# Exchanging two steps of ScalarE, relu and a small square root, in the expert loops of a mixture-of-experts kernel

## The chip, the cores and the metric
One core of one Trainium2 chip runs the whole program. The metric is the device time of one execution in microseconds, the median of several runs. The engines are TensorE (PE), VectorE (DVE), ScalarE (ACT), GpSimd (POOL) and SyncE (SP). Each goes through its own list of instructions in order; they are tied together by semaphores, which one engine raises and another waits for.

## The reference
The program is a layer of three stages on x of 8 x 256 tokens with 128 features: half an expert layer, an attention, and again half an expert layer (the same weights):

```python
x = x + 0.5 * ffn(layernorm(x))
x = x + attn(layernorm(x))
x = x + 0.5 * ffn(layernorm(x))
```

The expert layer has 8 experts, each token goes to the best 2 of them:

```python
h = relu(xt @ W1[e] + b1[e])            # 128 -> 512
h = layernorm(h) * g1[e] + be1[e]
y = relu(h @ W2[e] + b2[e])             # 512 -> 128
y = layernorm(y) * g2[e] + be2[e]
out = sum over the 2 experts of gate * y
```

All is float32. Each of the two normalisations needs 1 / sqrt(variance + eps) for each token. The square root is taken by ScalarE, the reciprocal by VectorE.

## The kernel before
**Tiles and pairs.** Tokens are sorted by expert into 39 tiles of 128 rows, each of one expert. Two tiles make a pair; there are 20 pairs (the last has one tile). Buffers are doubled: pair n uses slot u = n % 2. Both expert layers ("f1", first, and "f2", last) run this way. f1 does pair 0 and 1 by hand, pairs 2 to 15 in a hardware loop of two pairs a round (seven rounds), and pairs 16 to 19 unrolled. f2 has its first six pairs woven into the end of the attention by a hand-written order of their own (which the change doesn't touch), then the loop for pairs 6 to 15 (five rounds) and again 16 to 19 unrolled.

**What happens to a pair.** PE turns the two tiles of x (`turn_x`, line 829), multiplies by W1 (`hidden`, line 840, into PSUM), turns the relu's result in eight pieces (`turn_h`, line 849), and multiplies by W2 (`second`, line 858, 16 matmuls into bank 7). ScalarE evacuates PSUM and takes the roots: `copy_xT` (684), `relu` (691, one instruction of 1024 columns for the pair), `copy_hT` (697), `sqrt1` (701, the root of the variance of h), `sqrt2` (705, that of y), and `finish` (712, the last scaling of y into `yo`, two instructions). VectorE takes the statistics of the relu (`stats1`, 1192, two instructions; `moments1`, 1199), adds up y (`y_sums`, 1206 and 1209), clips y at zero and takes its statistics (`y_stats`, 1215 to 1221), and normalises it (`y_norm`, 1231 and 1233). In f1 SP stores `yo` and POOL gathers the tiles of x to come; in f2 SP loads the tiles and POOL scatters `yo`.

**The orders.** Each engine's order within one body is written by hand. For body n they are:

- PE: turn_h(n), turn_x(n+2), hidden(n+1), second(n)
- VectorE: moments1(n), y_sums(n-1), y_stats(n-1), y_norm(n-1), stats1(n+1)
- ScalarE: copy_hT(n), copy_xT(n+2), sqrt1(n), sqrt2(n-1), relu(n+1), finish(n-1)

**The waits around the change.** relu(n+1) waits for `h` (hidden(n+1) done), for `hTp` (turn_h(n-1) done, since it overwrites what was turned) and for `bn` (stats1(n-1) done). sqrt2(n-1) waits for `mv2` (y_stats(n-1) done). y_norm(n-1) waits for `sq2` (sqrt2(n-1)); finish(n-1) for `yz` (y_norm(n-1)) and for the store of two pairs ago; stats1(n+1) and turn_h(n+1) for `relu`. second(n) waits for `hTc` (copy_hT(n)) and for `ya` (y_sums(n-1) done, which frees bank 7). In f2 hidden(n+1) waits for relu(n), as there is but one set of banks for h; in f1 there are two.

At the head of a loop's round PE and VectorE read the numbers of the round's experts from SBUF into registers (`experts`, line 58); on PE this stands between the last matmul of second and the first wait of turn_h.

Of the kernel before, what the change touches and what calls it, by code (L numbers as in the profile page):

```python
# [106 lines left out]
def build(nc, x, Wq, Wk, Wv, Wo, lq1, lk1, lq2, lk2, Wr, br, W1, b1, g1, be1, W2, b2, g2, be2, out, stages=("f1", "at", "f2")):  # L107
    with ExitStack() as ctx:
# [433 lines left out]
        def turned_rows(act, S, g, first):  # L542

            act.wait_ge(S["xnTp"], g + 1)
            if g == 3:
                act.wait_ge(S["lgp"], 1)
            act.copy(turned_slot(g), turn_bank(g)[:].rearrange("p (a b) -> p a b", a=4)).then_inc(S["xnTc"], 1)
# [107 lines left out]
        def own_rows(act, h):  # L655

            act.wait_ge(s_wmix, h + 1)
            for a in range(4):
                e = 4 * h + a
                last = act.activation(wmix[0:16, e * DIM:(e + 1) * DIM], bank[6 + h][0:16, a * DIM:(a + 1) * DIM], ACT.Copy,  # L660
                                      scale=mask16[:, e:e + 1])
            last.then_inc(s_mixed, 1)

        def own_bias(act, a, b):
            for t in range(a, b):
                last = act.activation(be2x[:, t, :], be2p[:], ACT.Copy, scale=own_t[:, t:t + 1])
            last.then_inc(s_be2x, 1)

        def deviations(act, S, g, n=2):
            a, b = n * g, n * g + n  # L670
            act.wait_ge(S["mv"], b)
            act.activation(sdev[:, a:b], mv[:, a:b, 1], ACT.Sqrt, bias=eps_c[:]).then_inc(S["sd"], 1)
# [44 lines left out]
        def moe_scalar(act, S, first):  # L717
            if first:
                act.activation(spad, eps_c[:], ACT.Sqrt)

            if first:
                deviations(act, S, 0, 4)
                for g in range(1, 4):
                    deviations(act, S, g, 4)
                    turned_rows(act, S, g - 1, first)
                    if g == 1:
                        act.wait_ge(s_cols, 1)
                        act.copy(cols[:], bank[6][:, 0:96]).then_inc(s_colc, 1)
                        act.wait_ge(s_cols, 2)
                        act.copy(be2p[:], bank[7][:, 0:DIM]).then_inc(s_colc, 1)  # L730
                turned_rows(act, S, 3, first)
                hidden_weights_back(act, range(0, 3))
                act.wait_ge(s_ld_w2, 16)
                w2g = w2c[:].rearrange("p (a d) -> p a d", d=DIM)
                w2v = w2s[:].rearrange("p a c d -> p (a c) d")

                def scaled(h):
                    for a in range(16 * h, 16 * h + 16):
                        last = act.activation(w2g[:, a, :], w2v[:, a, :], ACT.Copy, scale=cols[:, a:a + 1])
                    last.then_inc(s_w2g, 1)  # L740

                scaled(0)
                hidden_weights_back(act, range(3, 6))
                scaled(1)
                act.wait_ge(S["top"], 1)
                act.activation(gden[:], mw[:], ACT.Exp).then_inc(S["gexp"], 1)
                act.wait_ge(A["lam"], 1)
                act.activation(lam_e[:], lam_s[:], ACT.Exp).then_inc(A["lame"], 1)
                act.activation(spad, eps_c[:], ACT.Sqrt)
                act.wait_ge(s_const, NCONST)  # L750
                own_rows(act, 0)
                hidden_weights_back(act, range(6, 8))

            def gates_turned():
                act.wait_ge(S["gTp"], 1)
                act.copy(gsT[:], gates_bank(first)).then_inc(S["gTc"], 1)

            if first:
                gates_turned()
            copy_xT, relu, copy_hT, sqrt1, sqrt2, finish = scalar_pair(act, S, first)  # L760

            def body(n, u, kx=2, kh=2, k=2, lag=True):
                copy_hT(n, u, k)
                if kx:
                    copy_xT(n + 2, u, kx)
                sqrt1(n, u, k)
                if lag:
                    sqrt2(n - 1, 1 - u)
                if kh:
                    relu(n + 1, 1 - u, kh)  # L770
                if lag:
                    finish(n - 1, 1 - u)

            if first:
                copy_xT(0, 0)
                own_rows(act, 1)

                def own_b2(h):
                    act.wait_ge(s_b2m, h + 1)
                    act.copy(b2p[:, 512 * h:512 * h + 512], bank[6 + h][:]).then_inc(s_mixed, 1)  # L780

                own_b2(0)
                relu(0, 0)
                own_b2(1)
                copy_xT(1, 1)
                own_bias(act, 0, 4)
                body(0, 0, lag=False)
                own_bias(act, 4, 10)
                body(1, 1)
                own_bias(act, 10, 16)  # L790
            with act.Fori(1 if first else AHEAD // 2, PAIRS // 2 - 2) as i:
                for u in range(2):
                    body(i * 2 + u, u)
            left = [min(2, max(0, SLOT_TILES - 2 * p)) for p in range(PAIRS + 2)]
            for n in range(PAIRS - 4, PAIRS):
                body(n, n % 2, kx=left[n + 2], kh=left[n + 1], k=left[n])
                if n >= LATE and first:
                    act.wait_ge(S["xnTp"], n - LATE + 5)
                    act.copy(late_oT[:, n - LATE].rearrange("p n e -> p (n e)"), bank[LATE_BANKS[n - LATE]][:, 0:LATE_TILES * P]
                             ).then_inc(S["xnTc"], 1)  # L800
            sqrt2(PAIRS - 1, (PAIRS - 1) % 2, left[PAIRS - 1])
            finish(PAIRS - 1, (PAIRS - 1) % 2, left[PAIRS - 1])
            if not first:
                gates_turned()
                gate_diagonals(act, (4, 5, 12, 13))
# [482 lines left out]
        def gates_bank(first):  # L1288
            return bank[5 if first else 1][:, 0:P]

        def gate_diagonals(eng, tiles):

            eng.wait_ge(sems["f2"]["gsum"], 1)
            for t in tiles:
                for k in range(TOPK):
                    g = gate[:, k, t:t + 1]
                    if eng is nc.scalar:
                        last = eng.activation(diag8[:, diag_at(t), k, :], ident[:], ACT.Copy, scale=g)
                    else:
                        last = eng.tensor_scalar(diag8[:, diag_at(t), k, :], ident[:], g, None, ALU.mult)  # L1300
            last.then_inc(s_diag, 1)
# [827 lines left out]
        def hidden_weights_back(act, experts_):  # L2129
            for e in experts_:  # L2130
                act.wait_ge(s_cols, 2 + e + 1)
                act.activation(w1s[:, e * FF:(e + 1) * FF], bank[W1_BANKS[e % 3]][:], ACT.Copy, scale=1.0 / P).then_inc(s_colc, 1)
# [165 lines left out]
```

## Time and profile before
| | |
|---|---|
| runs | 487.77, 489.46, 494.69 us (median 489.46) |
| profiled execution | span 487.7 us; no other time is given for it |
| PE busy | 424.1 us (87%), weight loads 289.9 us |
| VectorE busy | 351.3 us (72%) |
| ScalarE busy | 291.3 us (60%) |
| POOL busy | 255.2 us (52%) |
| line 691 (relu) | 40 instructions, 39.5 us |
| line 705 (sqrt2) | 40 instructions, 11.8 us; idle ahead of them 36.3 us, 25.6 of it until line 1221 of VectorE |
| chain that ended last | PE 44%, VectorE 19%, issue 14%, ScalarE 13% |

The busy share of an engine is over the whole span. "Idle ahead" is time in which the engine had nothing to do just before those instructions, and what is named with an arrow is what ended it, inferred from the semaphores. The chain that ended last is followed back from the last instruction. The f1 loop lies between 60 and 131 us, its unrolled pairs up to 149 us, the f2 loop between 400 and 447 us and its unrolled pairs up to 467 us.

### The profile page before, as it was taken

How to read it: one execution, taken by the hardware profiler on the slowest of the kernel's cores; microseconds unless marked ns; L12 is line 12 of the kernel's file. 1: busy time of each engine (PE TensorE's matmuls, PEld its weight loads, DVE VectorE, ACT ScalarE, POOL GpSimd, SP SyncE). 2: the span in 40 equal slices, each digit the busy share in tenths (PEclk: the TensorE clock that was granted, in tenths of full speed). 3: DMA queues.
4: the chain of work that ended last, by engine and by line, in shares of the span. 5: the costliest groups of instructions: out<-in, count | busy, mean ns of one | idle time of the engine just before them, and what ended most of it. 6: DMA issues, size and time to landing. Idle time of an engine off the chain costs nothing.

```text
span 487.7 us, 11940 instructions
## 1 busy us (share of the span) xinstructions
PE 424.1 (87%) x3686; PEld 289.9 (59%) x3693; DVE 351.3 (72%) x1291; ACT 291.3 (60%) x591; POOL 255.2 (52%) x355
## 2 busy tenths in 40 slices
PE   7999999999999678889897878786899689999883
PEld 7654667777776335556465554554566457776633
DVE  5874677877877595788967776555576848887765
ACT  2395876666654437778585757543755356676540
POOL 8684634343633567256473754546524828545430
PEclk9898999999999979999999989869899979999999
DMA  7901143354422101000000000101111111211017
GB/s 233 341 19 34 31 149 135 135 203 164 135 110 88 32 23 34 12 12 13 23 13 23 23 18 29 32 15 32 52 45 40 60 39 55 59 54 49 29 46 242
DMA packets 26001, 35.18 MB, mean 72 GB/s; under 512 B 4297, under 2 KB 18689, under 8 KB 24802
## 3 DMA queue, kind: packets, MB, share of 16 engines
q1 hardware_dynamic: 21010, 24.68, 15.3%
q0 software_dynamic: 4944, 9.90, 7.1%
q8 instruction: 26, 0.43, 0.4%
q14 instruction: 21, 0.17, 0.1%
HBM read 15.45 MB, written 18.30 MB: 69 GB/s over the span
## 4 chain that ended last, share of the span: by engine, by line
PE 44%; DVE 19%; issue 14%; ACT 13%; DMA 4%; DVEq 2%; SPq 1%; POOL 1%; another core or an unknown queue 1%; POOLq 0%; ACTq 0%
PE bank L840 5%; PE bank L858 4%; DVE mx L1930 4%; ACT wide L691 4%; ACT early L1488 3%; DVE st L1192 3%; PE bank L849 3%; PE bank L1684 2%; PE bank L1692 2%; ACT wide L1480 2%; PE bank L2126 2%; PE bank L1641 2%; PE bank L1702 2%; PE bank L1777 2%; PE bank L1663 2%
## 5 line engine op out<-in xcount | busy, mean ns | idle before, releaser
L858 PEld LDWEIGHTS bank<-w2c,hT 128*128 128x128 f32 x624 | 75.3, 194 | 27.0 <-issue 26.7
L858 PE MATMUL bank<-w2c,hT 128*128 x624 | 78.0, 278 | 6.4 <-ACT hT L697 3.3
L840 PE MATMUL bank<-w1s,xT 128*128 x156 | 75.9, 608 | 1.1 <-DVE w2c L2144 0.6
L1930 DVE TENSOR_REDUCE mx<-bank 128x4 f32<-128x1024 f32 (+1 forms) x48 | 58.6, 1221 | 21.8 <-PE bank L1672 17.9
L1488 ACT ACTIVATE early<-bank 128x768 f32<-128x768 f32 x64 | 51.8, 813 | 36.7 <-PE bank L1692 36.1
L484 POOL DMA_INDIRECT xgw<-xn_scratch,slot_u x39 | 37.1, 952 | 53.2 <-PE bank L829 43.2
L455 POOL DMA_INDIRECT y_scratch<-yo,dest_u x39 | 39.0, 1001 | 40.1 <-ACT yo L712 32.8
L1192 DVE BATCH_NORM_STATS2 st<-wide 128x6 f32<-128x512 f32 x78 | 50.1, 683 | 10.6 <-ACT wide L691 9.0
L697 ACT COPY hT<-bank 128x1024 f32<-128x1024 f32 (+1 forms) x40 | 39.5, 988 | 22.2 <-PE bank L849 19.7
L433 POOL DMA_INDIRECT xr_scratch<-row_buf,hi_i x32 | 31.9, 998 | 31.8 <-DVE hi_i L644 12.9
L849 PE MATMUL bank<-ident,wide 128*128 128x128 f32 x312 | 41.8, 276 | 5.2 <-ACT wide L691 4.2
L691 ACT ACTIVATE wide<-bank 128x1024 f32<-128x1024 f32 (+1 forms) x40 | 39.5, 988 | 8.1 <-PE bank L840 8.1
L849 PEld LDWEIGHTS bank<-ident,wide 128*128 128x128 f32 x312 | 34.2, 141 | 9.7 <-ACT wide L691 6.6
L840 PEld LDWEIGHTS bank<-w1s,xT 128*128 128x128 f32 x156 | 27.1, 194 | 21.1 <-issue 21.1
L1480 ACT COPY wide<-bank 128x1024 bf16<-128x1024 bf16 x32 | 32.2, 1014 | 8.9 <-PE bank L1641 8.8
L1361 POOL DMA_INDIRECT yk<-y_scratch,posi x28 | 28.0, 999 | 17.4 <-DMA yk<-y_scratch,posi 6.3
L1209 DVE SCALAR_TENSOR_TENSOR yy<-bank,r,b2p 128x128 f32<-128x128 f32 x78 | 24.7, 351 | 14.6 <-DVE r L1206 10.0
L705 ACT ACTIVATE sd<-mv,eps_c 128x2 f32<-128x2 f32 (+1 forms) x40 | 11.8, 296 | 36.3 <-DVE mv L1221 25.6
L1684 PE MATMUL bank<-mxT,sel 64*128 64x384 bf16 x128 | 22.6, 350 | 9.7 <-ACT early L1488 7.0
L712 ACT ACTIVATE yo<-yz,r 128x128 f32<-128x128 f32 x78 | 27.1, 394 | 5.7 <-DVE yz L1233 3.5
L1430 POOL TENSOR_TENSOR orr<-oms,neg_half 128x16 f32<-128x16 f32 x7 | 20.5, 2932 | 9.7 <-DVE oms L1967 9.5
L1663 PE MATMUL bank<-mrhs,mlhs 64*128 64x128 bf16 (+1 forms) x192 | 15.9, 246 | 10.6 <-DVE mx L1930 6.5
(360 smaller groups left out, 931.5 us busy)
## 6 DMA issues: line engine op xcount, KB each, us to landing
xr_scratch<-row_buf SPq DMA_DIRECT2D x8, 1032.0 KB
xgw<-xr_scratch SPq DMA_DIRECT2D x39, 64.5 KB
y_scratch<-yo SPq DMA_DIRECT2D x19, 128.0 KB
w1s<-in_L_ffn_W_dram SPq DMA_DIRECT2D x1, 2048.0 KB, 9.9
early<-y_scratch SPq DMA_DIRECT2D x8, 256.0 KB, 3.5
xn_scratch<-row_buf SPq DMA_DIRECT2D x1, 1024.0 KB
out_dram<-xs SPq DMA_DIRECT2D x8, 128.0 KB, 2.3
row_buf<-row_buf SPq DMA_DIRECT2D x6, 128.0 KB
```

What stands on the lines that cost most here:

```text
L455: pool.indirect_dma_start(out=y_dram, out_offset=bass.IndirectOffsetOnAxis(ap=dest_u[:, 2 * p + j:2 * p + j + 1], axis=0), in_=yo[:, p % 2 ...
L484: pool.indirect_dma_start(out=xg[:, u, :], out_offset=None, in_=xn_dram, in_offset=bass.IndirectOffsetOnAxis(ap=slot_u[:, n:n + 1], axis=0 ...
L691: act.activation(hh[:, u, 0:k, :], banks[:, h_at[u]:h_at[u] + k, :], ACT.Relu).then_inc(S["relu"], 1)
L697: act.copy(hT[:, u, 0:k, :], banks[:, 5:5 + k, :]).then_inc(S["hTc"], 1)
L840: last = pe.matmul(bank[h_at[u] + j][:], xT[:, u, j, :], w1s[:, bass.ds(e * FF, FF)], start=True, stop=True)
L849: last = pe.transpose(bank[5 + j][:, c * P:c * P + P], hh[:, u, j, c * P:(c + 1) * P], ident[:])
L858: last = pe.matmul(bank[7][:, j * DIM:(j + 1) * DIM], hT[:, u, j, c * P:(c + 1) * P], w2c[:, bass.ds(e * (FC * DIM) + c * DIM, DIM)], star ...
L1192: last = dve.bn_stats(st1[:, u, j, :], hh[:, u, j, :])
L1480: act.copy(dst[:, slot, :, u * P:u * P + P], src.bitcast(BF16).rearrange("p (a e) -> p a e", e=P)).then_inc(A[name + "Tc"], 1)
L1488: act.activation(prob[:, g], quad[:, low:low + 2, 0:3 * P], ACT.Exp).then_inc(A["prob"], 1)
L1684: pe.matmul(o, sel[r:r + 64, g:g + 1].to_broadcast([64, P]), mxT[r:r + 64, :], start=True, stop=False)
L1930: dve.tensor_reduce(mx[:, c:c + 2 * per].rearrange("p (a q) -> p q a", q=2), quad[:, low:low + 2, :].rearrange("p q (a e) -> p q a e", a=p ...
```

## The change
In the body that ScalarE runs for each pair, relu(n+1) goes ahead of sqrt2(n-1), and stands directly behind sqrt1(n). The orders of the other engines, all waits and all instructions stay as they are.

```diff
                 sqrt1(n, u, k)
-                if lag:
-                    sqrt2(n - 1, 1 - u)
                 if kh:
                     relu(n + 1, 1 - u, kh)
                 if lag:
+                    sqrt2(n - 1, 1 - u)
                     finish(n - 1, 1 - u)
```

`lag` is false in body 0 of f1 alone, `kh` is the number of tiles of pair n+1 and is 0 in the last body. Both steps stand together in bodies 1 to 18 of f1 and 6 to 18 of f2.

## Rows read from the trace of the kernel before

**Rows 1.** Windows, 69 to 130 us: length, then busy us: PE, PEld, DVE, ACT, POOL.
```profile
69.00:130.00 61.00, 58.12 (x372) 44.63 (x371) 48.21 (x209) 40.56 (x86) 23.70 (x28) 1.00 0.49 165
```

**Rows 2.** Timeline of ScalarE, first loop; start us, duration us, engine, line, operation.
```profile
104.71 0.30 ACT L705 ACTIVATE sd<-mv,eps_c 128x2 f32<-128x2 f32 x1 [0.80 <-DVE mv L1221]
104.91 1.00 ACT L691 ACTIVATE wide<-bank 128x1024 f32<-128x1024 f32 x1
...
109.67 0.29 ACT L705 ACTIVATE sd<-mv,eps_c 128x2 f32<-128x2 f32 x1 [1.09 <-DVE mv L1221]
109.88 1.00 ACT L691 ACTIVATE wide<-bank 128x1024 f32<-128x1024 f32 x1
110.83 0.69 ACT L712 ACTIVATE yo<-yz,r 128x128 f32<-128x128 f32 x2
```

**Rows 3.** Timeline of PE, same stretch, without weight loads.
```profile
102.37 1.88 PE L840 MATMUL bank<-w1s,xT 128*128 x4
104.09 1.95 PE L858 MATMUL bank<-w2c,hT 128*128 x16
105.97 1.09 PE L849 MATMUL bank<-ident,wide 128*128 128x128 f32 x8
...
108.84 1.95 PE L858 MATMUL bank<-w2c,hT 128*128 x16
111.23 0.95 PE L849 MATMUL bank<-ident,wide 128*128 128x128 f32 x7 [0.44 <-ACT wide L691]
```

**Rows 4.** Timeline of VectorE, same stretch.
```profile
105.23 0.61 DVE L1233 SCALAR_TENSOR_TENSOR yz<-yy,mv,g2b 128x128 f32<-128x128 f32 x2
105.95 1.28 DVE L1192 BATCH_NORM_STATS2 st<-wide 128x6 f32<-128x512 f32 x2
...
107.88 0.63 DVE L1209 SCALAR_TENSOR_TENSOR yy<-bank,r,b2p 128x128 f32<-128x128 f32 x2 [0.31 <-DVE r L1206]
...
109.49 0.15 DVE L1221 BATCH_NORM_AGGREGATE mv<-st 128x2 f32<-128x6 f32 x1
...
110.10 0.61 DVE L1233 SCALAR_TENSOR_TENSOR yz<-yy,mv,g2b 128x128 f32<-128x128 f32 x2
110.91 1.28 DVE L1192 BATCH_NORM_STATS2 st<-wide 128x6 f32<-128x512 f32 x2 [0.20 <-ACT wide L691]
```

**Rows 5.** Timeline of VectorE, end of the first loop.
```profile
130.16 0.94 DVE L1233 SCALAR_TENSOR_TENSOR yz<-yy,mv,g2b 128x128 f32<-128x128 f32 x2
131.03 0.68 DVE L1192 BATCH_NORM_STATS2 st<-wide 128x6 f32<-128x512 f32 x1
```

**Rows 6.** Timeline of ScalarE, four relus: two of the first loop, two of the last.
```profile
69.85 1.00 ACT L691 ACTIVATE wide<-bank 128x1024 f32<-128x1024 f32 x1
...
129.94 1.00 ACT L691 ACTIVATE wide<-bank 128x1024 f32<-128x1024 f32 x1
...
417.08 1.00 ACT L691 ACTIVATE wide<-bank 128x1024 f32<-128x1024 f32 x1
...
446.60 1.01 ACT L691 ACTIVATE wide<-bank 128x1024 f32<-128x1024 f32 x1
```

**Rows 7.** Timeline of PE, last loop, where PE has no gaps.
```profile
402.07 1.95 PE L858 MATMUL bank<-w2c,hT 128*128 x16
...
406.66 1.95 PE L858 MATMUL bank<-w2c,hT 128*128 x16
408.45 0.82 PE L849 MATMUL bank<-ident,wide 128*128 128x128 f32 x6
```

**Rows 8.** Timeline of PE, last loop, at a loop head.
```profile
425.89 1.95 PE L858 MATMUL bank<-w2c,hT 128*128 x16
428.05 0.52 PE L849 MATMUL bank<-ident,wide 128*128 128x128 f32 x3 [0.21 <-ACT wide L691]
```

**Rows 9.** Waits of PE, 60 to 141 us; us in total, times, longest us.
```profile
PE bank L849 <- ACT wide L691: 3.4, 7, 0.8
```

**Rows 10.** Waits of all engines, 407 to 448 us.
```profile
POOL y_scratch L455 <- ACT yo L712: 13.0, 7, 2.1
```

## The prediction
> **What bounds the kernel now.** Times are of one profiled execution with a span of 487.71 us; the three runs shown are 487.77, 489.46 and 494.69 us, so the span stands beside the lowest and 1.7 us under the median. I work out a difference on the trace and put it on the median.
>
> First the page's busy shares: TensorE (PE) is the busiest engine, 87% of the span. The stretch from 69 to 130 us lies inside the first expert loop, and there PE is busy for 58.1 of 61 us [rows 1]: whatever is moved on the other engines can bring little unless PE's own gaps close. Then the timeline of one round (two pairs), engine by engine. I call "h" the product of W1, "relu" line 691, "sqrt2" line 705, "stats1" line 1192 and "second" the product of W2, line 858.
>
> ScalarE: sqrt2 starts at 104.71 after 0.80 us of idleness, relu follows 0.20 later at 104.91 [rows 2]. PE: h of that pair starts at 102.37 and takes 1.88, so it is there at 104.25 [rows 3]. So relu stands 0.66 us behind a square root whose input comes late. No table load lies between the two: they start 0.20 apart [rows 2], so their exchange costs none. VectorE: the chain that sets the pace. stats1 starts at 105.95, the sums of y (line 1209) end at 107.88 + 0.63 = 108.51, the moments of y end at 109.49 + 0.15 = 109.64 [rows 4], and sqrt2 starts at 109.67 [rows 2]. After sqrt2 two ways lead to the next stats1, and they are almost equally long: through relu (109.88 + 1.00 = 110.88, stats1 at 110.91, for which VectorE stood idle 0.20) and through line 1233 (110.10 + 0.61 = 110.71) [rows 2, 4]. In the other pair of the round the second way ends at 105.23 + 0.61 = 105.84 against relu's 105.91 [rows 2, 4]. Taking relu out of the way therefore uncovers 0.07 to 0.17 us, not 1 us; with the 0.07 by which a stats1 may start before the end of line 1233 (131.03 against 130.16 + 0.94 = 131.10, [rows 5]) 0.14 to 0.24.
>
> How long is a round now: relu starts at 69.85 and, 12 pairs on, at 129.94: 60.09 / 6 = 10.01 us. In the last loop 417.08 and, 6 pairs on, 446.60: 29.52 / 3 = 9.84 us [rows 6].
>
> **The change part by part.** Nothing is added or removed. Relu and its three waits (h, the turned pair before last, its statistics) go ahead of sqrt2 and its one wait. No DMA is issued by this engine; SP's and POOL's queues are not passed.
>
> *Relu.* It can start 0.03 after h ends, 0.6 us sooner. Behind it on PE wait the transposes of line 849, but PE has to finish second first: without any gap, second to second takes 406.66 - 402.07 = 4.59 us and second to the transposes 408.45 - 406.66 = 1.79 us [rows 7]. Second started at 104.09, 0.16 before h's end by the trace [rows 3]. So what PE can win in this half of the round is 105.97 less 104.09 + 1.79, that is 0.09 us (105.97 is a little after relu's end at 105.91). In the other half the transposes start at 111.23 although relu ended at 110.88 [rows 2, 3]: 0.35 us after the semaphore. 108.84 + 1.79 = 110.63 is when PE is free; the 0.60 up to 111.23 is the head of the loop on PE's queue (the branch and the load of the expert numbers come there, in front of the wait), and an earlier relu doesn't shorten it. In the last loop it is 428.05 - 425.89 - 1.79 = 0.37 once [rows 8] and nothing at 408.45 [rows 7]; bounds 0 and 0.60, and for each loop I take its own steady row.
>
> The Trainium skill (Perfetto Trace Analysis, Optimization Strategy) says to take the busiest engine, find its gaps, and make what it waits for start sooner. The list of waits does name relu for 3.4 us of PE's idleness around the first loop, in 7 waits [rows 9]; by that rule the sum would be -3.4 us or, with the last loop, somewhat more. The releaser named had been done 0.35 us earlier in one such wait [rows 2, 3], so I give those microseconds to the loop head.
>
> *Sqrt2.* Now it is behind relu. An instruction behind relu starts at the earliest 0.95 after relu (109.88 to 110.83, [rows 2]). From the end of h: 0.03 + 0.95 to sqrt2, + 1.13 to the end of line 1233 (104.71 to 105.84), - 0.07 to stats1: VectorE's stats1 can't start before **h + 2.04**. Today it starts at 105.95, h + 1.70. Behind the held square root on ScalarE are the two scalings of yo, ended by h + 2.04 + 0.07 + 0.69 = h + 2.80, and behind them the copy of hT, which needs the transposes anyway (h + 1.63 + 1.06 = h + 2.69 at the earliest): it loses about 0.1 and has almost 1 us to spare before second. POOL, which sends yo, is idle for 13.0 us in 7 waits for it in the stretch shown [rows 10]: covered.
>
> *What the later stats1 holds up.* The y sums come 2.56 after stats1 (105.95 to 108.51), and second waits for them, since they read its bank. From the sums' end to second I have only 108.51 to 108.84 = 0.33 as an upper bound [rows 3, 4] (PE was just getting free then), and 0.03 (109.64 to 109.67, the moments to sqrt2) as the shortest hand-over as lower bound. I take 0.25, near the upper, because second must first work out an address. So second can't start before h + 2.04 + 2.56 + 0.25 = **h + 4.85**; PE alone would be there at h - 0.16 + 4.59 = h + 4.43. That is 0.42 us of a new wait on PE, in one half of each round; in the other half sqrt2 is released by the moments again (3.69 after stats1), since h is then early enough.
>
> *The new round.* 4.85 to the held second, 1.79 to the transposes, 2.80 + 0.16 to the end of h: 9.60 us plus the head. First loop 10.20 against 10.01: +0.19 x 6 = +1.1. Last loop, three steady rounds: 9.97 against 9.84: +0.4. The unrolled pairs at the loops' ends have no head: 4.80 each against 4.96 (105.95 to 110.91): -0.16 x 5 = -0.8 (two in the first loop's tail, three in the last's; the other pairs there carry extra work and I leave them). The way into each loop: one later square root that PE doesn't feel, 0. **Sum +0.7 us**: 488.4 for the profiled execution, 490.2 on the median. Bounds: with hand-over 0.03 a round loses 0.22 (some 11.5 rounds: -2.5), with 0.33 it gains 0.08 (+0.9); a head that runs while PE is held takes up to 0.42 off (-3.8 over the nine rounds that have one), a head of 0.60 in the last loop too +0.7.
>
> **The rivals.** *B, the wait on PE does not come*, or the loop head fits into it: then a round is 9.18 plus the head, or VectorE's own chain, 2 x (3.69 + 0.03 - 0.07) + 1.13 + 1.04 = 9.47 (1.04 is 109.67 to 110.71). First loop 9.78: -0.23 x 6 = -1.4; last 9.55: -0.29 x 3 = -0.9; tails -0.22 x 5 = -1.1; together -3.4: 486.1. For it: ScalarE idles 0.80 ahead of sqrt2 and relu's input lies ready. Against it: PE has hardly a gap of its own to give. The rule of the Trainium skill above (Perfetto Trace Analysis, Optimization Strategy) would end at the same time, by another way, and has its chance within B's.
>
> *C, slower:* the square root is held by a whole relu in every pair, since h never gets ahead of the y moments. Place: sqrt2, with VectorE's line 1233 and stats1 behind it. It decides from the point where h ends less than 0.95 us ahead of the moments in both halves; today it is 104.68 - 104.25 = 0.43 in this one (the moments end 0.03 before 104.71, as they do before 109.67 [rows 2, 4]). Price: a pair is then 3.69 + 0.03 + 0.95 + 1.13 - 0.07 = 5.73 against 5.00 (half of 10.01), +0.73 over some 32 pairs = +23 us, 513; if in every other pair, +12, 501. Against it: PE needs 4.59 for a pair, so h gains on such a slow VectorE in the very next pair, until the wait on the sums stops it.
>
> *D, nothing moves:* relu's gain and sqrt2's loss cancel to under 0.5 us, or relu gets no earlier: 489.5.
>
> **How the numbers follow.** A (sum above) 0.57, D 0.10, B 0.27, C 0.06. Predicted 490.2 us. The range 486.5 to 493.0 holds A with its bounds, D and about half of B; C and the rest of B are left out. A measurement of this kernel can tell about 2% (9.8 us) from no change: faster by more 0.03, which only several bounds together would give; slower by more 0.06, which is C; within 0.91.
>
> **What would show it.** In the profile after: relu starts within 0.1 us of h's end in both loops; ScalarE's idle time stands ahead of relu, no longer ahead of sqrt2; in one pair of two sqrt2 starts about 0.95 behind relu with the moments done long before; second (line 858) shows a gap of some 0.4 us in every other pair, released by line 1209; turned pairs no longer wait for line 691. Rounds of 10.2 us in the first loop would be A, 9.8 or less B, over 10.6 C. The prediction is wrong if second has no gap, or if the 0.60 at the loop head shrinks when relu is early.

## The result and the profile after

| | before | changed |
|---|---|---|
| runs beside each other | 487.77, 489.46, 493.57, 494.69 us | 491.97, 492.83, 497.91, 498.61 us |
| median | 491.51 us | 495.37 us |
| ratio | | 1.0131, 95% interval 1.0077 to 1.0185 |
| span of the profiled execution | 487.7 us | 496.2 us |
| PE busy | 424.1 us (87%) | 432.0 us (87%) |
| VectorE busy | 351.3 us (72%) | 348.1 us (70%) |
| idle ahead of stats1, VectorE | 10.6 us | 3.3 us |
| idle ahead of second, PE | 6.4 us | 10.2 us, 6.4 of it until the sums of y |

The ratio is taken over executions in the faster of the two states that this kernel shows, and is not the quotient of the two medians (1.0079, +3.9 us), which lies at the lower end of its interval. The change made the kernel slower: the value 1, no change, lies outside the interval, though the difference is under 2%. The times of the two profiled executions (8.5 us apart) are not the effect: what the loops say is below, and the attention between them scatters by several us in either kernel.

One round of the first loop, ScalarE's timeline of the changed kernel (start, duration, operation, idle time before it, in us). It answers to [rows 2]:

```profile
97.13 0.30 ACT L701 ACTIVATE sd<-mv,eps_c 128x2 f32<-128x2 f32 x1
97.81 1.02 ACT L691 ACTIVATE wide<-bank 128x1024 f32<-128x1024 f32 x1 [0.38 <-PE bank L839]
98.73 0.29 ACT L705 ACTIVATE sd<-mv,eps_c 128x2 f32<-128x2 f32 x1
...
102.40 1.02 ACT L691 ACTIVATE wide<-bank 128x1024 f32<-128x1024 f32 x1 [0.37 <-issue]
103.50 0.30 ACT L705 ACTIVATE sd<-mv,eps_c 128x2 f32<-128x2 f32 x1
```

The idle time stands ahead of relu now, and sqrt2 at 98.73 directly follows it. PE of the same round, answering to [rows 3]; line numbers from 769 on are one lower than before:

```profile
96.75 1.02 PE L839 MATMUL bank<-w1s,xT 128*128 x2
97.61 1.95 PE L857 MATMUL bank<-w2c,hT 128*128 x16
99.39 1.04 PE L848 MATMUL bank<-ident,wide 128*128 128x128 f32 x8
...
100.48 1.88 PE L839 MATMUL bank<-w1s,xT 128*128 x4
102.57 2.02 PE L857 MATMUL bank<-w2c,hT 128*128 x16 [0.20 <-DVE yy L1208]
105.16 1.06 PE L848 MATMUL bank<-ident,wide 128*128 128x128 f32 x8 [0.57 <-issue]
...
106.28 1.88 PE L839 MATMUL bank<-w1s,xT 128*128 x4
```

and VectorE, answering to [rows 4]:

```profile
97.61 0.15 DVE L1220 BATCH_NORM_AGGREGATE mv<-st 128x2 f32<-128x6 f32 x1
...
99.25 0.61 DVE L1232 SCALAR_TENSOR_TENSOR yz<-yy,mv,g2b 128x128 f32<-128x128 f32 x2
99.78 1.28 DVE L1191 BATCH_NORM_STATS2 st<-wide 128x6 f32<-128x512 f32 x2
...
101.70 0.63 DVE L1208 SCALAR_TENSOR_TENSOR yy<-bank,r,b2p 128x128 f32<-128x128 f32 x2 [0.31 <-DVE r L1205]
...
103.31 0.15 DVE L1220 BATCH_NORM_AGGREGATE mv<-st 128x2 f32<-128x6 f32 x1
```

Read the three together, from the end of h at 96.75 + 1.02 = 97.77. Relu goes at once, at 97.81. The square root of the pair before, whose moments had been ready at 97.61 + 0.15 = 97.76, waits for relu and starts at 98.73. Line 1232 ends at 99.86, stats1 starts at 99.78 (h + 2.01), the sums of y are there at 102.33, and second, for which PE stands idle 0.20, starts at 102.57 (h + 4.80, 0.24 after the sums). In the next half sqrt2 (103.50) follows its moments (103.46) and isn't held. PE's waits, 60 to 150 us (total, times, longest), say the same; they answer to [rows 9], where relu was named for 3.4 us in 7 waits between 60 and 141 us:

```profile
PE bank L848 <- issue: 4.3, 7, 1.0
PE bank L857 <- DVE yy L1208: 3.0, 8, 1.6
PE bank L848 <- ACT wide L691: 1.4, 1, 1.4
```

Relu has vanished as a releaser in all waits but one, and PE idles more than before: 4.3 us at the loop heads, for which relu had been named, and 3.0 us for the sums of y. 1.6 of these 3.0 are a single wait; in the changed kernel's execution of e12 (below) only seven waits of 0.2 us remain, 1.4 in all.

The Trainium skill (PSUM — Partial Sum Buffer, Engine vs sequencer instructions) says that the queues of ScalarE and VectorE are strictly first in, first out. The trace agrees: sqrt2 had its input at 97.76 and started at 98.73, 0.97 us later, behind a relu it has nothing to do with.

The last loop has the same held second. These lines of PE are from the changed kernel's execution of e12 and answer to [rows 8]:

```profile
386.54 1.88 PE L839 MATMUL bank<-w1s,xT 128*128 x4
388.62 2.02 PE L857 MATMUL bank<-w2c,hT 128*128 x16 [0.20 <-DVE yy L1208]
390.90 1.07 PE L848 MATMUL bank<-ident,wide 128*128 128x128 f32 x8 [0.27 <-issue]
```

Second to transposes is 2.28 us at this loop head, against 2.16 in [rows 8].

### The profile page after: what moved, and what is told of

It is laid out like the page before. It is cut to its first block, busy times and chain, and to the rows that moved or that the text cites. A ratio compares the mean times of both kernels' runs of the same rounds, so it can differ in the third digit from the quotient of the medians.

```text
span 496.2 us, 11940 instructions
## 1 busy us (share of the span) xinstructions
PE 432.0 (87%) x3686; PEld 295.0 (59%) x3693; DVE 348.1 (70%) x1291; ACT 292.4 (59%) x591; POOL 254.7 (51%) x355
## 4 chain that ended last, share of the span: by engine, by line
PE 60%; DVE 12%; issue 12%; ACT 8%; DMA 3%; POOL 1%; another core or an unknown queue 1%; SPq 1%; DVEq 1%; POOLq 0%
PE bank L839 10%; PE bank L857 9%; PE bank L848 5%; DVE mx L1929 4%; ACT early L1487 3%; PE bank L1683 3%; PE bank L1691 2%; PE bank L1701 2%; PE bank L1776 2%; PE bank L2261 2%; PE bank L1640 2%; PE bank L1624 2%; DVE st L1191 2%; PE bank L1794 2%; DMA early<-y_scratch 2%
## 5 line engine op out<-in xcount | busy, mean ns | idle before, releaser
L857 PE MATMUL bank<-w2c,hT 128*128 x624 | 79.5, 281 | 10.2 <-DVE yy L1208 6.4
L839 PE MATMUL bank<-w1s,xT 128*128 x156 | 74.1, 596 | 1.3 <-issue 0.6
L455 POOL DMA_INDIRECT y_scratch<-yo,dest_u x39 | 39.0, 999 | 38.2 <-ACT yo L712 30.9
L691 ACT ACTIVATE wide<-bank 128x1024 f32<-128x1024 f32 (+1 forms) x40 | 40.1, 1002 | 18.1 <-PE bank L839 9.1
L1683 PE MATMUL bank<-mxT,sel 64*128 64x384 bf16 x128 | 23.8, 368 | 10.3 <-ACT early L1487 7.1
L1429 POOL TENSOR_TENSOR orr<-oms,neg_half 128x16 f32<-128x16 f32 x7 | 20.5, 2932 | 10.9 <-DVE oms L1966 10.6
L1230 DVE RECIPROCAL r<-sd 128x2 f32<-128x2 f32 (+1 forms) x40 | 6.5, 163 | 26.9 <-issue 13.6
```

The lines of the kernel that those rows point to most:

```text
L455: pool.indirect_dma_start(out=y_dram, out_offset=bass.IndirectOffsetOnAxis(ap=dest_u[:, 2 * p + j:2 * p + j + 1], axis=0), in_=yo[:, p % 2 ...
L691: act.activation(hh[:, u, 0:k, :], banks[:, h_at[u]:h_at[u] + k, :], ACT.Relu).then_inc(S["relu"], 1)
L839: last = pe.matmul(bank[h_at[u] + j][:], xT[:, u, j, :], w1s[:, bass.ds(e * FF, FF)], start=True, stop=True)
L857: last = pe.matmul(bank[7][:, j * DIM:(j + 1) * DIM], hT[:, u, j, c * P:(c + 1) * P], w2c[:, bass.ds(e * (FC * DIM) + c * DIM, DIM)], star ...
L1683: pe.matmul(o, sel[r:r + 64, g:g + 1].to_broadcast([64, P]), mxT[r:r + 64, :], start=True, stop=False)
```

## The experiments

From here on I measure by stages of the profiled executions, one for each kernel. Over these the loops and the ways out repeat to some 0.3 us where the total doesn't: "first loop" is relu 4 to relu 16 of the first expert layer (six rounds), "way out" relu 16 to the first yo of pair 19, "last loop" is relu 8 to relu 16 of the last layer (four rounds), "end" from the last layer's first yo of pair 19 to the end of the span. All are starts on ScalarE, read from its timeline (lines 691 and 712). The executions of the first table of stages had a mean granted PE clock of 0.93 to 0.97; those of the second and third, on two other chips, had 0.98 to 0.99 and took some 27 us less, nearly all of it in the attention and in the first pairs of the last layer. So the tables are not compared with each other outside the loops.

### Repetitions, and each layer alone

The control is the kernel before, and the second run the changed kernel, each unchanged. For one layer alone the body of ScalarE tests which layer it is in. This is e3 against the kernel before; e4 has `ahead = not first`:

```diff
-                if lag:
+                ahead = first
+                if lag and not ahead:
                     sqrt2(n - 1, 1 - u)
                 if kh:
                     relu(n + 1, 1 - u, kh)
+                if lag and ahead:
+                    sqrt2(n - 1, 1 - u)
                 if lag:
                     finish(n - 1, 1 - u)
```

> The kernel before once more, unchanged. It tells how far the attention between the two expert layers scatters by itself. Theory 1 (the change works in the expert loops alone: +3.35 us from relu 1 to relu 19 of the first layer, -1.6 us from relu 6 to relu 19 of the last, and the other microseconds are scatter): the loops repeat to 0.3 us (90.8 and 65.5), the stretch between them moves by several us and so does the granted clock in it. Theory 2 (the change also makes the attention about 4 us longer): the stretch between the loops is again near 251.7 us.

> The changed kernel once more. Theory 1: first loop's relus 94.1 us, last loop's 63.9 us, the stretch between them anything from 251 to 256 us, total +1.8 us against before (492 or so, ratio 1.004). Theory 2: the stretch near 255.5 again, total +6 us (ratio 1.013).

> Relu ahead of the square root in the first expert layer alone. Theory 1: first layer's relus 94.1 us, last layer's as before, 65.5; total +3.4 us (ratio 1.007), the worst of the variants. Theory 2, where the attention pays since it starts later: +7 us (1.015).

> Relu ahead of the square root in the last expert layer alone. Theory 1: first layer as before, 90.8 us; last layer's relus 63.9 us against 65.5; total -1.6 us (ratio 0.997), below the kernel before. Theory 2: the attention runs ahead of every instruction that is moved here, so it is as before, and the total is -1.6 as well; if the last layer is slower by itself, +1 or more.

| | first loop | way out | between the layers (yo 19 to relu 0) | last loop | way out | end | ratio to before, 95% |
|---|---|---|---|---|---|---|---|
| before | 60.09 | 22.59 | 203.3 | 39.35 | 23.14 | 18.0 | |
| e1 before again | 60.06 | 22.58 | 201.5 | 39.63 | 23.13 | 21.0 | 0.9983 (0.9936 to 1.0030) |
| changed | 62.47 | 23.56 | 207.9 | 40.01 | 23.78 | 19.3 | 1.0131 (1.0077 to 1.0185) |
| e2 changed again | 62.61 | 23.57 | 202.9 | 40.12 | 23.80 | 19.2 | 1.0129 (1.0032 to 1.0227) |
| e3 first layer alone | 62.70 | 23.54 | 198.5 | 39.36 | 23.14 | 18.6 | 1.0061 (1.0008 to 1.0114) |
| e4 last layer alone | 60.07 | 22.58 | 205.1 | 40.11 | 23.79 | 19.4 | 1.0044 (0.9997 to 1.0091) |

The loops are slower exactly where the exchange is: first loop +2.4 to +2.6 us and way out +0.97, last loop +0.4 to +0.8 and way out +0.65. The attention doesn't follow: it is shortest (198.5) in a kernel with the exchange and 202.9 in the changed kernel's second execution, near the control's 201.5. Theory 2 falls by this stage, though the total of e2, 1.0129, is the one that it gave (1.013), and not the 1.004 of Theory 1: Theory 1 had the place right and the sum wrong. The interval of e4 just includes no change, so that the last layer's loss rests on its stages. The way into the first loop, relu 1 to relu 4, took 15.5 us before and 17.0 in e1, so relu 1 to relu 19 did not repeat to the 0.3 us that I expected (90.8 and 92.2). My expectation that the last layer gains 1.6 us failed too, and the reason is in the choice of the marker: relu 19 comes early in the changed kernel, but yo of pair 19 doesn't. I had taken the pace of the relus for the pace of the layer. At the loop's start the marker works the other way: relu 8 comes early too, which makes the stage from it look longer. From relu 6, the last one that the change doesn't move, to the last yo it is 72.9, 73.3 and 73.0 us with the order of before (before, e1, e3) and 73.5, 74.2 and 74.3 with relu first (changed, e2, e4).

In the execution of e1 "end" was 21.0 us with the order of before, so it has two lengths in one and the same kernel; what the exchange adds to it I read from the last table.

### PE's loop heads taken off the path

The first layer's seven rounds are written out on PE alone, and the expert numbers of the next round are loaded ahead of the odd pair's second; e5 has the order of before, e6 that of the change. Arithmetic and waits are the same, and the last layer keeps its loop. The main lines, with gaps marked:

```diff
+                nxt = load() if load else None
                 second(n, u, e[0:k])
+                return nxt
...
-            with pe.Fori(1 if first else AHEAD // 2, PAIRS // 2 - 2) as i:
-                e = experts(pe, eid, i * 4, 6)
-                for u in range(2):
-                    body(i * 2 + u, i, u, e[2 * u:])
...
+            if first:
+                e = experts(pe, eid, 4, 6)
+                for i in range(1, PAIRS // 2 - 2):
+                    more = (4 * i + 4, 6) if i < PAIRS // 2 - 3 else (2 * PAIRS - 8, 7)
+                    body(2 * i, i, 0, e)
+                    e = body(2 * i + 1, i, 1, e[2:], load=lambda: experts(pe, eid, *more))
```

> Order as before (square root, relu). PE's seven rounds of the first expert layer are written out and the next expert numbers are loaded ahead of the odd pair's second, so the 0.6 us of the loop head are gone from PE's path; the other engines keep their loops. Measured by relu 4 to relu 16 (60.1 us now, twelve pairs). Theory H (relu first is slow only because a held second and the loop head are paid one after the other): before's round is set by VectorE's chain and the relu, not by the head, so it hardly moves: 59.4 to 60.1. Rival R (before's round is bound by PE's head): 56.5 to 58.

> The same PE program without loop heads, with relu ahead of the square root. Now 62.5 us from relu 4 to relu 16 with the heads of 0.8. Theory H: a round is 4.80 + 1.79 + 3.00 = 9.59, so 57.6 us, below before's order in the same program: the sign turns. Rival S (the wait of second on the sums of y costs by itself, whatever the head): it stays above before's order, 60.5 us or more.

### Two banks for y

In the last layer's loop, PSUM bank 0 is free; y of even pairs goes there, and second waits for the sums of the pair before last. VectorE reads y from the same bank. These are PE's lines, with the ends of the long ones left out:

```diff
-                    pe.wait_ge(S["ya"], n)
+                    pe.wait_ge(S["ya"], n - 1 if two and not isinstance(n, int) else n)
...
-                        last = pe.matmul(bank[7][:, j * DIM:(j + 1) * DIM], ...
+                        last = pe.matmul(bank[0 if two and u == 0 else 7][:, j * DIM:(j + 1) * DIM], ...
```

> Relu first, and in the last expert layer's loop y of even pairs goes to PSUM bank 0, of odd pairs to bank 7, so that second waits for the sums of the pair before last. Relu 8 to relu 16 is 40.1 us with one bank, 39.4 to 39.6 in the kernel before. Theory H: second's gap of 0.2 to 0.4 us per round goes, and a round is PE's 9.18 plus a head of 0.4 to 0.6, about 9.6: 38.2 to 38.9 us. Rival T (what slows the loop is VectorE, which starts its statistics later behind the held square root, not PE's wait): 40.0 as with one bank.

> Two banks for y as in the run beside it, with the order of before. Theory H: second doesn't wait there for the sums to any length, the loop stays at 39.3 to 39.6 us from relu 8 to relu 16. If the address work behind that wait was on PE's path after all, 38.9 to 39.2.

| order | first loop, head on the path | first loop, head off | last loop, one bank | last loop, two banks |
|---|---|---|---|---|
| before | 60.04 (e8) | 59.88 (e5) | 39.36 (e5) | 39.35 (e8) |
| changed | 62.41 (e7) | 58.20 (e6) | 40.11 (e6) | 37.53 (e7) |

Both turn the sign of the exchange in their loop. With the order of before neither repair does anything to speak of (0.2 and 0.0 us). That fits a round which VectorE's chain with the relu in it sets there; in e5 PE's waits for relu between 60 and 150 us are down to 1.1 us (3.5 before), and the loop is as long. With relu first the repairs take 4.2 us (the head, first loop) and 2.6 us (the banks, last loop) off. Each of these kernels was timed once, so the whole times say little: e5 462.27, e6 461.18, e7 463.48, e8 461.56 us, the kernel before beside them 461.32. PE of e6, one round:

```profile
98.58 2.00 PE L857 MATMUL bank<-w2c,hT 128*128 x16
100.42 1.04 PE L848 MATMUL bank<-ident,wide 128*128 128x128 f32 x8
...
103.58 2.05 PE L857 MATMUL bank<-w2c,hT 128*128 x16 [0.19 <-issue]
105.47 0.71 PE L848 MATMUL bank<-ident,wide 128*128 128x128 f32 x5
```

Second to transposes is 1.84 and 1.89 us where the changed kernel has 1.78 and 2.59 (102.57 to 105.16). The small gap ahead of second is still there; it costs little by itself. What cost in the first loop was the gap and then the head, one behind the other. 58.20 is a little above the expected 57.6 (9.70 a round, not 9.59). And PE of e7, last loop, where the gap is gone:

```profile
400.59 1.95 PE L857 MATMUL bank<-w2c,hT 128*128 x16
402.53 1.06 PE L848 MATMUL bank<-ident,wide 128*128 128x128 f32 x8
...
405.37 1.95 PE L857 MATMUL bank<-w2c,hT 128*128 x16
407.15 1.04 PE L848 MATMUL bank<-ident,wide 128*128 128x128 f32 x8
```

Its 37.53 us are below the 38.2 that I expected: 9.38 a round by the relus, near PE's own 9.18. The heads are still in this loop, and between 380 and 410 us they cost 0.15 us (402.53 - 400.59 - 1.79) or nothing, where behind a held second it was 0.49 (2.28 - 1.79). Measured by the starts of stats1 the same eight pairs take 37.93 us, 9.48 a round, which is the 9.47 that the prediction had worked out for VectorE alone: it falls 0.4 us behind the relus in four rounds. Rivals R, S and T fall.

### Half a round each, the best version, and the change again

e10 and e11 put relu first in one half of the loops' rounds, and in all unrolled pairs (`u == 0`, e10, shown below, issues the odd pair's relu; `u == 1`, e11, the even pair's). e9 is the changed kernel with both repairs, the written-out PE rounds in the first layer and the two banks in the last.

```diff
+                ahead = u == 0 or (isinstance(n, int) and n >= PAIRS - 4)
-                if lag:
+                if lag and not ahead:
                     sqrt2(n - 1, 1 - u)
                 if kh:
                     relu(n + 1, 1 - u, kh)
+                if lag and ahead:
+                    sqrt2(n - 1, 1 - u)
                 if lag:
                     finish(n - 1, 1 - u)
```

> Relu first in both expert layers, PE's loop heads taken off the path in the first and two PSUM banks for y in the last. By the stage lengths of the runs that had one of the two: the first layer from relu 1 to the last yo 96.2 us (97.7 before), the last from relu 6 to the last yo 71.3 (72.9), the stretch behind it 0.4 longer: -2.7 us, ratio 0.994. If the two loops are not independent (the first layer's end moves the attention's start), anything between 0.99 and 1.00.

> Inside the loops only the relu of the odd pair (the first half of a round) goes ahead of the square root; in the unrolled pairs as in the changed kernel. Theory H (the loss is one held square root a round, the one behind the odd pair's relu): 62.0 to 62.7 us from relu 4 to relu 16, as with both. Rival U (each of the two exchanges costs its share): 61.3.

> Only the relu of the even pair (the second half of a round) goes ahead in the loops. Theory H: this square root is released by the moments of y and not held, VectorE's half becomes 4.7 instead of 4.96, and PE's 9.18 plus head of 0.6 = 9.78 is the bound: 58.7 to 60.0 us, at or below before's 60.1. Rival U: 61.3.

> The changed kernel again beside these, to weigh the whole against the stages. By the stage lengths so far: first layer +3.5 (r4 to r16 +2.5, from there to the last yo +1.0), last layer +1.3, behind it +1.0 to +1.5: together +5.5 to +6.5 us, ratio 1.012 to 1.014, however fast the attention is on this chip.

| | first loop | way out | last loop | way out | end | ratio to before, 95% |
|---|---|---|---|---|---|---|
| before's order (e8) | 60.04 | 22.59 | 39.35 | 23.14 | 17.8 | |
| e10 odd relu first | 62.87 | 22.27 | 40.16 | 22.77 | 19.4 | one run |
| e11 even relu first | 59.93 | 22.93 | 39.72 | 23.60 | 19.7 | one run |
| e12 changed | 62.47 | 23.57 | 40.04 | 23.82 | 19.2 | 1.0062 (1.0029 to 1.0094) |
| e9 both repairs | 58.23 | 22.95 | 37.44 | 23.95 | 18.1 | 0.9899 (0.9862 to 0.9937) |

The whole loss of the first loop sits in the odd pair's exchange (62.87, even a little over the 62.7 I allowed), none in the even pair's (59.93). Rival U falls. PE of e10 has the held second and the longer head behind it (103.22 - 100.64 = 2.58):

```profile
100.64 2.02 PE L861 MATMUL bank<-w2c,hT 128*128 x16 [0.20 <-DVE yy L1212]
103.22 0.96 PE L852 MATMUL bank<-ident,wide 128*128 128x128 f32 x7 [0.56 <-ACT wide L691]
```

But the even pair's exchange wins nothing either, at the upper end of what I expected: PE's loop head stands in that half, as this timeline of e11's PE shows (99.63 to 102.03 is 2.40, as in [rows 3]).

```profile
99.63 1.95 PE L861 MATMUL bank<-w2c,hT 128*128 x16
102.03 1.06 PE L852 MATMUL bank<-ident,wide 128*128 128x128 f32 x8 [0.46 <-issue]
```

e9 is the best of all kernels here: 456.85 us against 462.22 for the kernel before on the same chip, 1.0% less with an interval of 0.6 to 1.4. I had expected -2.7 us, and it is -4.7 (+-1.8); its stages against e8 account for -1.6 in the first layer (relu 1 to the last yo), -1.7 in the last (relu 6 to the last yo) and +0.2 at the end. Both repairs together with the order of before were not run; e5 and e8 have one each.

e12 fell short of its expectation: +2.9 us (1.3 to 4.3), where its stages sum to +2.4 (first loop), +1.0, +0.7, +0.7, +1.3 = +6.1. Two parts of the difference can be read from the traces. One comes back between the layers; that the attention starts on what the first pairs have stored, and so hides some of the delay, would explain it, but no run shows it. From relu 1 of the first layer to relu 0 of the last it is 279.1 us in e8 and 281.3 in e12, +2.3 for stages that add up to +3.4. The other is a stretch that the table leaves out, relu 6 to relu 8 of the last layer: 10.37 us in e8 and 9.67 in e12, since relu 8 is itself an earlier relu. So the last layer costs +0.7 from relu 6 to its last yo (72.9 and 73.5) and not the +1.4 of its two stages. What is left, some +4.2 us, is at the upper end of the interval.

## Why the prediction was wrong

I forecast +0.7 us, 490.2, within 486.5 to 493.0; measured are 495.37 us and +1.3%. Of the 5.2 us between the two, 2.05 are the base: the median of the kernel before was 489.46 when I forecast and 491.51 with the fourth run. The rest is the effect, +3.9 us by the medians and +6.4 by the ratio, where I had +0.7: three microseconds and more that the sum lacks.

**What was right.** Relu at h + 0.03 (0.04 measured), sqrt2 held behind it (0.92, predicted 0.95), stats1 at h + 2.04 (2.01), second at h + 4.85 (4.80), the hand-over to second 0.25 (0.24), one held square root a round and not two. Relu was not what PE waited for at the first loop's heads: it is now ended 1.74 us ahead of those transposes (103.42 against 105.16) and they start no earlier after second. (With the head gone it is the next thing to wait for: in e5 the transposes still start 2.1 us after second.) The rule of the Trainium skill (Perfetto Trace Analysis, Optimization Strategy), applied to the releaser that the view names, would have promised -3.4 us; the measurement decides against it here. The releaser was only the last semaphore in front of a queue that still had the loop head to do: with the head off the path, second to transposes is 1.89 us instead of 2.59 (e6).

**The first failed step is the size of the head, in "9.60 us plus the head. First loop 10.20 against 10.01".** I kept the head of 0.60 from a round in which PE had not been held. Behind a held second it is 0.80: 102.57 to 105.16 is 2.59, less 1.79. With 3.00 instead of 2.96 to the next h, the round is 4.80 + 2.59 + 3.00 = 10.39, and six rounds measure 62.47 / 6 = 10.41 against my 10.20 and 10.01 before: +2.4 us instead of +1.1. The last loop measures 40.01 against 39.35 over four rounds, +0.7 instead of my +0.4 over three; a round there costs 0.17, close to my 0.13, and I had counted one round too few. That a held second and the head behind it are what costs is shown by e5 and e6 for the first loop; for the last loop e7 and e8 show that it is the held second, with which its head shrinks too. Why the head grows by 0.2 is not shown, as these views don't show what PE's queue does in it.

**The second is the term of the unrolled pairs and the ways in and out, -0.8 and 0.** I reckoned 4.80 per pair against 4.96 by the relus. The relus do come faster (14.35 us for the last three against 15.17), but a layer ends with y. Today stats1 starts 1.09 after relu (131.03 and 129.94, [rows 5, 6]); in the changed kernel 2.05, by these rows of ScalarE and VectorE:

```profile
133.56 1.02 ACT L691 ACTIVATE wide<-bank 128x1024 f32<-128x1024 f32 x1 [0.37 <-PE bank L839]
```
```profile
135.61 1.28 DVE L1191 BATCH_NORM_STATS2 st<-wide 128x6 f32<-128x512 f32 x2
```

The 0.96 by which VectorE trails has to be paid at the end of the layer: +0.97 and +0.65 us on the ways out, where I had written -0.8 for both. Counted from stats1 of pair 16, the ways out are 21.50 and 21.51 us in the first layer and 22.10 and 21.74 in the last (before, changed): the unrolled pairs gain nothing in the one and 0.36 us in the other. The number stood in my own working (h + 2.04 against h + 1.70 plus the relu's 0.6 that moved); I didn't carry it to the end of the layer. The way in, which I had put at 0, is +0.0 in the first layer (relu 1 to relu 4, 15.17 and 15.21 in e8 and e12) but -0.7 in the last (relu 6 to relu 8), so that there trailing and earlier relus cancel.

Together: +2.4 + 0.7 in the loops and +1.6 on the ways out are +4.7 us, to which the end adds 1.3 (19.2 against 17.8 in e12 and e8), while 0.7 go off on the way into the last loop and 1.1 of the first layer's 3.4 between the layers. That leaves some +4.2, inside the interval of the first ratio (+3.8 to +9.1 us) and inside that of e12 (+1.3 to +4.3). So the mechanism of case A was the right one, with its head and its ways in and out mis-sized; the 1.3 us at the end of the kernel were in no term at all. B's conditions, no wait on PE or no head behind it, are what the two repairs bring about, and with them its sign comes true. C never came near: sqrt2 is held in one half only.

**What stays open.** The stretch behind the last yo took 18.0, 21.0, 18.6, 17.8 and 17.8 us with the order of before in the last layer (before, e1, e3, e5, e8). With one bank and relu first in all or half of the rounds it took 19.0 to 19.7 in all seven executions, and with two banks 18.1 and 18.2 (e9, e7). The kernel before, e1, e8 and e12 do the same in its first 9 us (PE is busy for 6.8 us in 26 instructions in each); the difference lies behind them, where the DMA engines were busy for 0.70, 0.54, 0.70 and 0.61 of the time and PE's granted clock was 0.97, 0.85, 1.00 and 0.80 of full speed. I made no run on it, and the cause stays open. The way into the first loop took 15.5 and 17.0 us (relu 1 to relu 4) in two executions of the same kernel.

## What to carry to other kernels

Moving ready work ahead of a step that waits costs that step nothing only if its own input arrives no earlier than the work ends, in every phase of the loop: here 1.0 us of relu went ahead of a 0.3 us root whose consumer sat on the loop's longest chain. Follow the held step around the loop until it meets the engine you meant to feed, and ask which buffer makes that engine wait; one more PSUM bank in one loop and a loop head off the path in the other turned the same exchange, in runs made together, from +0.6% into -1.0%, and neither shortened its loop by more than 0.2 us without it. And measure a stage between instructions that the change leaves alone, at its start and at its end, not at the one that was moved.

## What the runs showed of the hardware

The same kernel took 488.9 us in the median of 29 runs on one chip, 461.3 in a single run on a second and 462.2 in the median of 14 on a third; chip and time of the run changed together, so which of the two it was stays open. The mean granted clock of PE was 0.954 of full speed in the profiled execution of the kernel before and 0.989 in that of e8, which has the same order of ScalarE; from the end of the first layer to the first relu of the last one it was 203.3 us against 181.3, and the six pairs behind it 41.0 against 35.7, while the loops, at full clock in both, took 60.09 and 60.04, 39.35 and 39.35 us. A head of a hardware loop that loads a register from memory on PE cost, in the first loop, 0.6 us where second ran freely and 0.8 where it was held, and 0.1 where it was written out with the load ahead of 16 matmuls; in the last loop 0.37 in [rows 8], up to 0.49 behind the held second of e12 and 0.15 or less in e7.
